# Expert layers of a decoder: a fourth, narrower copy of the up products

## The reference, cut to what matters

```python
logits = x @ Wg.T
top_v, top_i = jax.lax.top_k(logits, K)                    # K = 2 of E = 8
...
exp_batches = jnp.zeros((E, cap, d)).at[flat_e, pos_safe].set(x[tok], mode='drop')   # cap = 1280
h = jnp.einsum('ecd,edf->ecf', exp_batches, W1)            # up: 512 -> 2 x 1024
inp, gate = jnp.split(h, 2, axis=-1)
h = jax.nn.gelu(inp, approximate=False) * gate
exp_out = jnp.einsum('eci,eid->ecd', h, W2)                # down: 1024 -> 512
```

## Time and profile before

| | |
|---|---|
| time, median of 3 runs | 1478.99 us (1477.98 to 1485.1) |
| the profiled execution's own time | 1480.64 us |
| its span, first to last instruction | 1478.7 us |
| mean granted clock of TensorE | 0.989 |
| TensorE busy | 1436.5 us, 97% of the span |
| VectorE, ScalarE, GpSimd busy | 44%, 40%, 25% |
| mean transfer rate | 92 GB/s |

### The profile page before, as it was taken

How to read it: one execution, slowest core, us unless ns; L and a number is a source line. 1 busy time by engine, 2 the same in 40 slices (tenths; PEclk the granted TensorE clock), 3 DMA queues, 4 the chain that set the end, 5 groups by cost and what they waited for, 6 DMA issues and landing times.

```text
span 1478.7 us, 22298 instructions
## 1 busy us (share of the span) xinstructions
PE 1436.5 (97%) x7508; PEld 1214.7 (82%) x7509; DVE 654.9 (44%) x1454; ACT 593.2 (40%) x1018; POOL 375.4 (25%) x366
## 2 busy tenths in 40 slices
PE   6999999989989999999999999999999999999997
PEld 5768887777876988888889888899889888898886
DVE  7535666657887563122523421166323420253111
ACT  5535554258776653213523421155323421252212
POOL 3402233127666422103202111121302112021111
PEclk9999999999997999999999999999999999999999
DMA  9410221218648864103515522155504412052112
GB/s 206 59 64 29 86 86 58 86 33 209 165 138 207 186 182 112 24 20 71 146 53 112 115 64 35 16 162 178 136 13 108 112 57 43 7 151 55 21 35 28
DMA packets 80679, 135.62 MB, mean 92 GB/s; under 512 B 31059, under 2 KB 31187, under 8 KB 79605
## 3 DMA queue, kind: packets, MB, share of 16 engines
q1 hardware_dynamic: 63252, 97.66, 23.9%
q0 software_dynamic: 17376, 37.30, 13.4%
HBM read 94.41 MB, written 40.53 MB: 91 GB/s over the span
## 4 chain that ended last, share of the span: by engine, by line
PE 91%; DVE 4%; ACT 2%; issue 1%; DMA 1%; POOL 1%; SPq 0%; POOLq 0%; DVEq 0%; ACTq 0%
PE pg L1054 16%; PE pg L1055 16%; PE pg L1056 16%; PE pj L1054 10%; PE pj L1056 10%; PE pj L1055 10%; PE pj L1293 2%; PE pg L1321 2%; PE pt L1462 2%; PE pg L1259 2%; PE pt L1280 1%; DMA out_rows<-ost,etab 1%; PE pt L1075 1%; DVE kf L1586 1%; PE pt L1205 1%
## 5 line engine op out<-in xcount | busy, mean ns | idle before, releaser
L1054 PE MATMUL pg<-xe_hi,w_hi 128*128 128x512 f32 (+2 forms) x1152 | 402.2, 349 | 1.9 <-DVE xe_lo L1538 1.9
L1056 PE MATMUL pg<-xe_hi,w_lo 128*128 128x512 f32 (+2 forms) x1152 | 401.6, 349 | 0.0
L1055 PE MATMUL pg<-xe_lo,w_hi 128*128 128x512 f32 (+2 forms) x1152 | 401.6, 349 | 0.0
L2012 DVE TENSOR_TENSOR hp<-gl,pg 128x512 f32<-128x512 f32 x136 | 93.6, 688 | 569.8 <-ACT gl L1025 569.7
L732 POOL DMA_INDIRECT out_rows<-ost,etab x62 | 99.1, 1599 | 720.8 <-ACT ost L1009 358.7
L1025 ACT ACTIVATE gl<-pg 128x512 f32<-128x512 f32 x136 | 81.4, 598 | 410.8 <-PE pg L1056 410.8
L1054 PEld LDWEIGHTS pg<-xe_hi,w_hi 128*128 128x128 f32 x1152 | 219.2, 190 | 27.7 <-issue 1.4
L1055 PEld LDWEIGHTS pg<-xe_lo,w_hi 128*128 128x128 f32 x1152 | 219.2, 190 | 25.0
L1056 PEld LDWEIGHTS pg<-xe_hi,w_lo 128*128 128x128 f32 x1152 | 219.1, 190 | 25.0
L1054 PE MATMUL pj<-w_hi,hg_hi 128*128 128x512 f32 x448 | 177.1, 395 | 0.0
L1056 PE MATMUL pj<-w_hi,hg_lo 128*128 128x512 f32 x448 | 174.5, 390 | 0.0
(11 more groups left out here) (260 smaller groups left out, 2016.2 us busy)
## 6 DMA issues: line engine op xcount, KB each, us to landing
stage<-w SPq DMA_DIRECT2D x96, 512.0 KB, 4.0
xr<-x SPq DMA_DIRECT2D x8, 1024.0 KB, 9.0
out_rows<-xr SPq DMA_DIRECT2D x8, 1024.0 KB, 6.8
x_rows<-xn SPq DMA_DIRECT2D x8, 1024.0 KB, 7.8
x_in<-x SPq DMA_DIRECT2D x7, 1024.0 KB, 5.3
x_rows<-zrow POOLq DMA_DIRECT2D x1, 2304.0 KB, 8.5
late_xT<-xT_hi SPq DMA_DIRECT2D x2, 1024.0 KB, 3.8
late_xT<-xT_lo SPq DMA_DIRECT2D x2, 1024.0 KB, 5.9
```

What stands on the lines that cost most here:

```text
L1054: nc.tensor.matmul(o, lh, rh, start=start, stop=False)
L1055: nc.tensor.matmul(o, lh, rl, start=False, stop=False)
L1056: return nc.tensor.matmul(o, ll, rh, start=False, stop=stop)
L2012: v.tensor_tensor(hp[j % 2][:], gl[j % 2][:], pg[:, 2 + j % 2, :], ALU.mult).then_inc(s_hp, 1)
```

## The change

The list `UP_WIDTHS` now holds the widths, 224, 256, 384 and 512 columns, and `up` takes the number of columns itself. A small recursive function writes a binary tree of branches: first `left < 257`, then in the one arm `left < 225` and in the other `left < 385`. Everything else is as it was; the soon part still has 256 columns.

```diff
+UP_WIDTHS = [2 * P - 32, 2 * P, 3 * P, 4 * P]
...
-                    def up(tiles):
-
-                        w = tiles * P
+                    def up(w):
+
                         pe.wait_ge(s_xelo, following)
...
-                    with pe.If(left < 2 * P + 1):
-                        up(2)
-                    with pe.Else():
-                        with pe.If(left > 3 * P):
-                            up(4)
+                    def up_narrowest(widths):
+
+                        if len(widths) == 1:
+                            up(widths[0])
+                            return
+                        half = len(widths) // 2
+                        with pe.If(left < widths[half - 1] + 1):
+                            up_narrowest(widths[:half])
                         with pe.Else():
-                            up(3)
+                            up_narrowest(widths[half:])
+
+                    up_narrowest(UP_WIDTHS)
```

## The result

The kernel became slower: 1505.67 us (median of 5 runs, 1493.87 to 1512.84) against 1478.99 before, a ratio of 1.016 with a 95% interval of 1.013 to 1.019. The forecast was 1484.4 us in a range from 1474 to 1491, so the sign was right and the size far too small. A second measurement of the same kernel gave 1507.34 (1496.37 to 1515.61, 6 runs), ratio 1.018 (1.014 to 1.023).

A forecast was written before the change was run, and what follows sets the result against it. TensorE, busy for 97% of the span, was taken as the bound. -5.2 (narrow products) + 10.4 (fetch misses) + 0.15 (first exit) = +5.4 us on the profiled 1480.64; as a median 1484.4 us, range 1474 to 1491.

The forecast's parts named there:

- The narrow products: Up stages of three passes: 224-column products take 111 ns instead of 120, paced by weight loads, gaining 5.2 us.
- The bounds of 106.7 and 120: Time in ns of a 224-column up product: 7.7 us gained if only columns count, nothing if weights need 120.
- the rival that they don't gain: Up products: weights need 120 ns, sum +10.6, 1489.6 us; no gain or a loss in the product, chance 0.06.
- Nothing else late: Narrow passes: ScalarE, VectorE, gathered rows and weight pieces keep up with the shorter pieces; costed at nothing.
- The fetch is the loss, and what a miss costs: Loop's instruction fetch: a miss costs 3.3 us more, 0.95 shown on the way in; eleven make 10.4 us.
- The rival with room for the longer loop: Instruction buffer holds the four-copy loop; only the first jump to the 512 copy misses anew: 1475.1 us, chance 0.27.
- the rule of where a packet is put: Instruction buffer of eight places: a missed packet goes behind the one fetched ahead; eleven passes miss once on their way in.
- The second entry and the way out: Pass entries that miss cost 0.95 us each; the first pass's exit pause grows from 1.80 to 1.95 us, +0.15.
- The second rival: Sixteen passes miss on the way in, seven also on the way out: +22.6 us, 1501.6 us, chance 0.12.

The follow-up runs named there:

- six_shifted: six_aligned with 50 instead of 65 never executed products ahead of the loop, which starts 30 instructions earlier: 1480.75 us, ratio 1.002.
- narrow_three_copies: Kernel before the change, still three copies, the narrowest 224 columns wide for all five chunks up to 256 rows, some products left out: 1472.91 us, ratio 0.996.
- dead_256: Kernel before the change plus 128 never executed products (258 instructions) at the loop's end: 1563.83 us, ratio 1.059.
- six_aligned: Kernel before the change with six of eight narrow pieces at 224 columns and 65 never executed products ahead of the loop: 1548.07 us, ratio 1.046.
- five_of_eight: Kernel before the change with the first five of eight narrow pieces at 224 columns, the rest shared with the 256 copy: 1490.08 us, ratio 1.008.
- dead_60: Kernel before the change plus 30 never executed products (62 instructions) at the loop's end: 1480.77 us, ratio 1.000.

## Why the prediction was wrong

- *The narrow products*: right. 111 ns forecast from the pace of the weight loads, 111.6 measured. The bounds of 106.7 and 120 are out, and so is the rival that they don't gain. That the load sets this pace is argued and was not tested; the trace of before bears on it: eight transposes of 128 columns, each with a load of its own, take 0.88 us there (L1462 at 549.73), 0.11 each, with little more than half the columns.
- *Nothing else late*: right. In the loop TensorE waits for nothing but instructions and, for 0.8 us before and after alike, for `xe_lo`; ScalarE, VectorE and the gathers kept up.
- *The fetch is the loss, and what a miss costs*: right. Packets of 256 instructions, eight places, some 3.2 us to a miss, 0.95 of it shown; 1.0 was measured. The rival with room for the longer loop is out: eight packets touched and a ninth fetched ahead do not fit, while seven and one ahead do (six_shifted). The Trainium skill (Runtime: NRT & Kernel Launch, section Instruction fetch mechanics) gives TensorE 128 KiB, refilled in blocks of 16 KiB, from which eight follow; with eight the runs agree. With the "current 2-page window" of the same section they don't: a loop that touches seven packets is not fetched again behind its second pass.
- *The step that failed is the rule of where a packet is put, and with it the count of misses.* I had a jump that misses put its packet "behind the one fetched ahead", and walked the seventeen passes by it: eleven passes that miss on their way in, four of them at the 512 copy, two at the 256 copy, five at the head. In the trace all sixteen passes behind the first do, fifteen at the head and the second pass at the 512 copy: 15 us and 3.9 us, where the sum has 10.4. What fits the fetches of before and of after is simpler: a packet has its place by its number, modulo eight, and only a jump that comes while a fetch is under way puts its packet behind that one (so I took for the rule what the earlier trace rows show as the exception). Then the ninth packet lies on the first in every pass, and the first is needed in every pass. That this is the rule of the places is inferred from the packets' times and from the kernels above that it fits; no row names a place.
- *The second entry and the way out*. I priced each entry alike, 0.95 us; the second pass's jump takes 6.3 us and shows 3.9. The way out of the first pass was sized at +0.15 us by its one row of before and measured +3.1: by the count of instructions the common rest of the loop now begins some thirty before a packet's end, and behind the first miss a second packet is late (2.9 us).
- *The clock* had no term in the sum. In this trace pauses of 1 us did not bring it down; those of 2 to 4 us were followed by stretches at 1.2 GHz, about 3 us of the loop in the profile, and the other runs have lower clocks. A pause's length alone does not decide: behind 1.77 us in narrow_three_copies the clock fell (540.0 to 543.4 us), behind 1.80 in before and 2.4 and 2.5 in dead_256 (at 701 and 988 us) it did not.
- The second rival had the number of entries that miss right, sixteen, and its 1501.6 us is the nearest time. The time is partly luck: it holds 12.6 us for misses on the way out of seven copies, of which only the first pass's came, and its 1.8 us was already in the time before.

With 18.9 for the misses on the way in instead of 10.4, 3.1 for 0.15 on the way out and 3 for the clock, the terms make -4.8 + 18.9 + 3.1 + 3 = 20.2, the profile's difference.

## What to carry to other kernels

A loop of an engine's program has a size in instruction packets, and the one fetched ahead counts. Before a copy of code is added to a loop, count its packets from the start of the packet in which it begins, and look whether the trace shows any instruction packet after the first passes. If it ends a little beyond the room, moving its start by some never executed instructions ahead of it can be worth more than the optimization. And price a pause by what is queued, but add the clock where it lasts some microseconds.

## What the hardware showed that I had not expected

- Code that is never executed can cost 84 us (dead_256, 5.9%), and 30 instructions of position 67 us (six_aligned against six_shifted).
- A jump back right behind the entry into the packet too many is worse than one that comes later: 1548 us (six_aligned, some 20 instructions into it) and 1564 (dead_256, which jumps over its dead code to the last few), against 1490 with some 80 (five_of_eight) and 1506 with some 230 (after). A jump right behind the call for another packet took up to 5.0 us in dead_256 and 6.3 in after (two transfers 0.2 us apart) instead of 3.2.
- The time of one program varies with the clock that it is granted: the 23 runs of before beside dead_60 go from 1472.94 us at a mean of 0.995 over 1479.95 at 0.989 to 1486.62 at 0.984.
